# A Mamba front spread over two chunks, its narrow products in column groups, and every scaling with C on GpSimd

## What is computed

```
xz = h @ W_in;  xm, z = split(xz, 2)
xm = silu(causal_conv(xm, conv_w, 4 taps) + conv_b)
dtr, Bm, Cm = split(xm @ W_xp, [64, 80])        # 64 + 16 + 16 columns
dt = softplus(dtr @ W_dt + b_dt);  A = -exp(A_log)
def step(hst, (dt_t, B_t, C_t, x_t)):            # 64 steps, one after the other
    hst = hst * exp(dt_t * A) + (dt_t * x_t) * B_t     # 128 x 512 x 16
    y   = einsum('bds,bs->bd', hst, C_t)
y = (ys + xm * D_param) * silu(z);  out = x + gate * (y @ W_out)
```

## Time and profile before

| | us |
|---|---|
| median of 3 runs | 2333.99 (2333.95 to 2335.63) |
| the profiled execution's own time | 2334.89 |
| its span in the profile | 2333.1 |
| first keep of the scan starts | 620.30 |
| last feed of the scan starts (two in the row) | 2264.66 |

### The profile page before, as it was taken

The page is one execution under the profiler, slowest core; times in us unless marked ns, Lnnn a source line. Parts: engine busy times, 40 slices in busy tenths (PEclk is TensorE's granted clock), DMA queues, the critical chain, the costliest instruction groups (busy, mean ns, idle before and its releaser), DMA issues. The chain is left out here.

```text
span 2333.1 us, 44474 instructions
## 1 busy us (share of the span) xinstructions
PE 2051.4 (88%) x13497; PEld 1579.0 (68%) x13497; DVE 1969.4 (84%) x3686; ACT 1688.3 (72%) x3652; POOL 1635.2 (70%) x1800
## 2 busy tenths in 40 slices
PE   4899999995699999999999999999999999999870
PEld 3566666662467777777777777777777778777760
DVE  2788888884299898989889898989989898988983
ACT  0455555552688888898888879898888979888840
POOL 2799999985667676776767677776767677676530
PEclk8999999996699999999999999999999999999995
DMA  5122212211000000000000000000000000000218
GB/s 142 39 64 64 64 62 63 62 49 36 10 1 19 6 15 6 15 15 6 15 5 19 6 15 8 13 15 6 20 6 15 6 15 15 6 6 6 95 69 288
DMA packets 71471, 80.75 MB, mean 35 GB/s; under 512 B 12227, under 2 KB 63619, under 8 KB 69188
## 3 DMA queue, kind: packets, MB, share of 16 engines
q1 hardware_dynamic: 66052, 69.52, 9.3%
q10 hardware_dynamic: 5184, 8.39, 1.0%
HBM read 44.33 MB, written 33.55 MB: 33 GB/s over the span
## 5 line engine op out<-in xcount | busy, mean ns | idle before, releaser
L632 ACT ACTIVATE decay<-dtT,decay_rate 128x256 f32<-128x256 f32 x2048 | 866.5, 495 | 0.2
L527 PE MATMUL bank<-ident,decay 128*128 128x128 f32 x4096 | 622.4, 275 | 101.6 <-ACT decay L632 56.0
L537 PEld LDWEIGHTS bank<-ident,scaled 128*128 128x128 f32 x4096 | 486.2, 142 | 231.6 <-issue 193.1
L537 PE MATMUL bank<-ident,scaled 128*128 128x128 f32 x4096 | 622.8, 275 | 1.5 <-POOL scaled L452 1.4
L527 PEld LDWEIGHTS bank<-ident,decay 128*128 128x128 f32 x4096 | 471.7, 141 | 143.7 <-ACT decay L632 103.7
L452 POOL TENSOR_SCALAR scaled<-state,bc 128x512 f32<-128x512 f32 x384 | 278.2, 730 | 255.9 <-DVE state L752 209.3
L742 DVE TENSOR_TENSOR bank<-bank,state 128x512 f32<-128x512 f32 x512 | 340.8, 691 | 117.7 <-PE bank L527 111.5
L452 POOL TENSOR_SCALAR scaled<-fresh,bc 128x512 f32<-128x512 f32 x384 | 273.5, 717 | 235.0 <-DVE fresh L752 214.3
L742 DVE TENSOR_TENSOR bank<-bank,fresh 128x512 f32<-128x512 f32 x512 | 340.3, 690 | 58.9 <-PE bank L527 55.4
L752 DVE SCALAR_TENSOR_TENSOR fresh<-dtx,bc,bank 128x512 f32<-128x512 f32 x512 | 356.9, 737 | 0.0
L752 DVE SCALAR_TENSOR_TENSOR state<-dtx,bc,bank 128x512 f32<-128x512 f32 x512 | 356.8, 737 | 0.0
(11 more groups left out here) (139 smaller groups left out, 3617.0 us busy)
## 6 DMA issues: line engine op xcount, KB each, us to landing
xt<-in_x_dram SPq DMA_DIRECT2D x64, 128.0 KB, 2.2
resid<-x SPq DMA_DIRECT2D x64, 128.0 KB, 1.8
normed<-xh SPq DMA_DIRECT2D x64, 128.0 KB, 1.7
xg<-normed SPq DMA_DIRECT2D x64, 128.0 KB, 2.1
ssm_out<-yo SPq DMA_DIRECT2D x32, 256.0 KB, 2.0
fin_r<-resid SPq DMA_DIRECT2D x8, 1024.0 KB, 13.2
mask_bc<-in_mask_BxS_ik_dram SPq DMA_DIRECT2D x64, 64.0 KB, 2.9
fin_y<-ssm_out SPq DMA_DIRECT2D x32, 128.0 KB, 3.0
```

What stands on the lines that cost most here:

```text
L527: mm = pe.transpose(dec_bank[i % DECAY_BANKS][:, m * P:(m + 1) * P], decay[:, i // BLOCK % 2, n % GROUP, m, t % HALF * P:(t % HALF + 1) * ...
L537: mm = pe.matmul(y_bank[t % HALF][:, m * P:(m + 1) * P], scaled[:, i % RING, m * P:(m + 1) * P], ident[:, :], is_transpose=True, start=Fal ...
L632: act.activation(decay[:, block % 2, e // CB, m, :], dtT[par][:, m, half * HTOK:(half + 1) * HTOK], ACT.Exp, scale=decay_rate[:, m, n:n + ...
```

## The change

- `ON_SCALAR` is empty: all 64 scalings of a chunk are POOL's, none ACT's.
- The front of chunk k runs through bodies k - 2 to k. A position in `SLOTS` is 64 times the body, counted from k - 2, plus the slot. Body k - 2 now holds h0, h1 and u0 to u3 in slots 51 to 60 (before 0 to 10 of body k - 1), and the first of the taps, which start in slot 57 on POOL and 62 on DVE (before 6 and 10) and run on into slots 0 to 4 of body k - 1.
- The rest of body k - 1: gating of x in slots 3, 6, 7, 10; dtr in 9 and 13 with out1 between; dt in 16, 20, 25, 29 with bcT and bc between; ln of softplus in slot 31, its POOL part in 33 to 40; z in 32 to 41 (before 14 to 21); x0 to x3 in 46 to 50; tanh of z in 52 (before 55). The gating of z on POOL moves to slots 5 to 15 of body k.
- dtr was 4 products of 64 columns in a row. It is now 2 x 2: two products of one slot write the lower and the upper half of the partitions, and `w_dt`, stacked twice, adds the halves up within the dt products, whose contraction is now 128 deep instead of 64.
- bc was 16 products with xs as weights and 32 columns streaming. Now four products of 32 output rows each (bcT, two a slot, 512 columns) write four partition groups of a side bank, ACT moves them to SBUF, and four products with `eye_sum` (four stacked unit matrices) turn and add them (bc).
- tanh of x goes into dtT instead of `tmp`. There is one more small DMA of W_dt and one more small DVE instruction (`eye_sum`) in the set-up.
- There is one more body without a scan, c = -2, which makes h and u of chunk 0; body -1 makes the rest of chunk 0 and then h and u of chunk 1.

```diff
-ON_SCALAR = (3, 7, 11, 15)
+ON_SCALAR = ()
...
-        SLOTS = dict(zip(JOBS, ((0,), (1,), (3, 4), (5, 6), (7, 8), (9, 10), (11, 12, 13),
-                                (14, 15), (16, 17), (18, 19), (20, 21),
-                                (22, 23, 24, 25), (27,), (29,), (31,), (33,), (35, 36, 37, 38),
-                                (42, 43, 44), (48,), (50,), (52,), (54,))))
+        SLOTS = {"dtr": at(B1, 9, 13), "out1": at(B3, 10, 11, 12), "dt0": at(B1, 16), "bcT": at(B1, 17, 18),
+                 "dt1": at(B1, 20), "bc": at(B1, 22, 23), "dt2": at(B1, 25), "dt3": at(B1, 29),
+                 "z0": at(B1, 32, 33), "z1": at(B1, 34, 35), "z2": at(B1, 37, 38), "z3": at(B1, 39, 41),
+                 "out0": at(B2, 42, 43, 44), "x0": at(B1, 46), "x1": at(B1, 48), "x2": at(B1, 49), "x3": at(B1, 50),
+                 "h0": at(0, 51), "h1": at(0, 52), "u0": at(0, 53, 54), "u1": at(0, 55, 56),
+                 "u2": at(0, 57, 58), "u3": at(0, 59, 60)}
...
-        X_ORDER, X_TANH, X_GATE = (0, 2, 3, 1), (13, 16, 18, 20), (15, 17, 19, 21)
-        MODULATE, CARRY, SOFTPLUS, GATES = (28, 33), 24, 38, 56
+        X_ORDER, X_TANH, X_GATE = (0, 2, 3, 1), at(B1, 1, 4, 5, 8), at(B1, 3, 6, 7, 10)
+        MODULATE, CARRY, LN = at(0, 21, 25), B1 + 18, B1 + 31
+        SOFTPLUS = at(B1, *range(33, 33 + 2 * CB))
+        Z_TANH, Z_GATES = B1 + 52, at(B2, 5, 6, 8, 9, 11, 12, 14, 15)
...
                 elif kind == "dtr":
+                    pe.wait_ge(s_xs, k * CB + 2 * piece + 2)
+                    for g in range(P // DTR):
+                        m = X_ORDER[2 * piece + g]
+                        mm = pe.matmul(side[g * DTR:(g + 1) * DTR, :], w_xp[:, m, 0:DTR], x[:, m, :],
+                                       start=(piece == 0), stop=(piece == pieces - 1), skip_group_check=True)
+                elif kind == "bcT":
+                    for g in (2 * piece, 2 * piece + 1):
+                        mm = pe.matmul(side[g * 2 * DS:(g + 1) * 2 * DS, :], w_xp[:, g, DTR:DTR + 2 * DS],
+                                       x[:, g, :], start=True, stop=True, tile_position=(0, g * 2 * DS))
+                elif kind == "bc":
+                    for t in (2 * piece, 2 * piece + 1):
+                        mm = pe.matmul(side[:, t * 2 * DS:(t + 1) * 2 * DS], bcT[:, t * P:(t + 1) * P], eye_sum[:, :],
+                                       start=True, stop=True)
```

More of the change, by code:

```diff
@@ L256, in build @@
         s_out = sem("out_stored")
-        JOBS = ("h0 h1 u0 u1 u2 u3 out1 z0 z1 z2 z3 "
-                "dtr dt0 dt1 dt2 dt3 bc out0 x0 x1 x2 x3").split()
-        SLOTS = dict(zip(JOBS, ((0,), (1,), (3, 4), (5, 6), (7, 8), (9, 10), (11, 12, 13),
-                                (14, 15), (16, 17), (18, 19), (20, 21),
-                                (22, 23, 24, 25), (27,), (29,), (31,), (33,), (35, 36, 37, 38),
-                                (42, 43, 44), (48,), (50,), (52,), (54,))))
-        POOL_TAPS = [(m, k) for m in (0, 1) for k in range(TAPS - 1)]
@@ L296, in side_turn, with at @@
-        def side_turn(c, job):
-            return product(c, job) % 2, product(c, job) // 2
-        def side_of(c, job):
-            return side_bank[side_turn(c, job)[0]]
-        def filled(eng, c, job):
-            eng.wait_ge(s_side_filled, product(c, job) + 1)
-        def moved(eng, c, job):
-            b, turn = side_turn(c, job)
+        B1, B2, B3 = ITEMS, 2 * ITEMS, 3 * ITEMS
+        def at(start, *slots):
+            return tuple(start + s for s in slots)
+        SLOTS = {"dtr": at(B1, 9, 13), "out1": at(B3, 10, 11, 12), "dt0": at(B1, 16), "bcT": at(B1, 17, 18),
[4 more added lines that the diff above has]
+                 "u2": at(0, 57, 58), "u3": at(0, 59, 60)}
@@ new lines, in build, with chunk_at @@
+        ROWS = {"out1": B3 + 12, "out0": B2 + 44}
+        BODIES = range(-2, CHUNKS + 1)
+        def chunk_at(c, i, position):
+            k = c + 2 - position // ITEMS
+            return k if position % ITEMS == i and 0 <= k < CHUNKS else None
+        SEQUENCE, COMPLETED = {}, {}
+        for c in BODIES:
+            for i in range(ITEMS):
+                for job in SLOTS:
+                    first, last = chunk_at(c, i, SLOTS[job][0]), chunk_at(c, i, SLOTS[job][-1])
+                    if first is not None:
+                        SEQUENCE[job, first] = len(SEQUENCE)
+                    if last is not None:
+                        COMPLETED[job, last] = len(COMPLETED)
@@ L399, in prefetch_resid @@
                         .then_inc(s_fin_r, 16)
-            def body(c, par, post, scan, pre):
-                if pre and c + 2 < CHUNKS:
-                    filled(sp, c, "h1")
-                    apart(sp)
-                    gather(c + 2)
-                if post:
+            for c in BODIES:
+                if scanned(c - 1):
                     store_rows(c - 1, 1)
@@ L409, in body @@
                     prefetch_resid()
-                if scan:
+                if scanned(c):
                     store_rows(c, 0)
-            body(-1, 1, False, False, True)
-            body(0, 0, False, True, True)
-            for c in range(1, CHUNKS + 1):
-                body(c, c % 2, True, c < CHUNKS, c < CHUNKS - 1)
+                if c + 3 < CHUNKS:
+                    filled(sp, c + 2, "h1")
+                    apart(sp)
+                    gather(c + 3)
             final_rows(sp, 0)
@@ L517, in mamba_tensor @@
+            for c in BODIES:
+                for i in range(ITEMS):
+                    slot(c, i)
         def mamba_tensor(pe):
@@ L618, in mamba_tensor, with slot @@
-            mamba_bodies(pe, body)
+            SKIPS = [index_of(0, t) + LAG - 1 for t in range(T)]
+            def slot(c, i):
+                if i + 2 < ITEMS:
+                    if scanned(c):
+                        turn_decay(c, i + 2)
+                elif scanned(c + 1):
+                    turn_decay(c + 1, i + 2 - ITEMS)
+                if scanned(c) and i in SKIPS:
+                    skip_term(c, SKIPS.index(i))
+                for job in SLOTS:
+                    for piece, position in enumerate(SLOTS[job]):
+                        k = chunk_at(c, i, position)
+                        if k is not None:
+                            fill(k, job, piece)
+                if i >= LAG and scanned(c):
+                    sum_state(c, i - LAG)
+                if i < LAG and scanned(c - 1):
+                    sum_state(c - 1, i - LAG + ITEMS)
```

463 lines of the change are left out of this document (232 added, 231 removed).

## The result

| | before | after |
|---|---|---|
| median, us | 2334.81 (2333.95 to 2338.54, 4 runs) | 2355.49 (2351.51 to 2358.59, 4 runs) |
| the profiled execution's own time, its span | 2334.89, 2333.1 | 2358.59, 2356.8 |
| first keep of the scan starts | 620.30 | 636.67 |
| period of a chunk | 103.9 | 105.1 |

The ratio is 1.0085, with an interval of 1.0064 to 1.0105. The changed kernel is 0.9% slower, 20.7 us. The forecast was 2335, with "slower" as the likeliest sign. 2355 lies inside the whole range (2304 to 2378), but 3 us above the one that the forecast case had for itself (2318 to 2352).

The account below looks back on a forecast made before the run. PE's path in slots 10 to 62, then DVE's heavy stretch, would bound the kernel: 2333.1 - 4.5 - 5.8 - 2.1 + 13 = 2333.7 us span, forecast 2335, range 2304 to 2378.

Parts of the forecast that it names:

- the forecast case: Whole kernel: ACT's wait goes, a PE wait of the same size replaces it; 2335 us, range 2318 to 2352, chance 0.64.
- two rivals that did not happen: Column-group products running in sequence, 2378 us, chance 0.11; POOL becoming the last engine, 2365 us, chance 0.10.
- What bounds the kernel, and the new place of the wait: Keeps wait 8.9 us a chunk, the largest part through ACT; afterwards 8 to 10 for PE, in slots 32 to 61.
- Column groups: Narrow products dtr and bcT: two run side by side at one product's cost; PE's work falls 3.6 us a chunk.
- one after the other: Rival: paired narrow products on PE run in sequence, 2.9 us a chunk more, 43 in all, 2378 us; chance 0.11.
- The charge of 1.15: PE's price in us for a slot with two narrow products, 1.00 + 0.09 + 0.06, mode switches included.
- The wait of u0 for h1: Slot 53: PE's u0 waits 1.7 us for ACT's move of h1, behind the tanh of z.
- the term of 13: Start-up before the first keep: 13 us more, about 5 for bcT and bc, 8 for h, u and two taps.
- DVE's heavy stretch, slots 62 to 7: DVE's pairs, taps and gates take 22.2 us while PE has no fill; item 63's turn comes 1.15 us late.
- the 103.1 of the links: Chunk period summed as 2.5 + 75.5 + 1.7 + 1.15 + 22.2 = 103.1 us, taken as 103.6 for lateness.
- Scalings on POOL cost nothing: Sixteen more scalings, 11.7 us a chunk, bring POOL to 86 of 104 us; cost taken as nothing.
- The rival of a DVE nearly unbound: Cheaper column groups and an early tanh shorten PE's path by 1.7 + 1.8 us; 2282 us, chance 0.15.

Follow-up runs that it names:

- the third run: The changed kernel with states 3, 7, 11 and 15 scaled on ACT again, nothing else: 2414.42 us, ratio 1.0336.
- An order that comes near it: The changed kernel with tanh of z in slot 53, DVE's taps in slots 58 to 63 and out0 in slots 61 to 63: 2256.47 us, ratio 0.9666.
- the first placing of the groups: The kernel before with column groups alone, dtr in slots 22 and 25, bcT in 35 and 36, bc in 38 and 39: 2382.9 us, ratio 1.0203.

## Why the prediction came out as it did

By its steps, the changed kernel's profiled execution against a forecast span of 2333.7: it is 2356.8, 23.1 more. First keep: forecast 633.3, measured 636.7, 3.4 of it. The scan from first keep to last feed makes up the other 19.7, nearly all of it in the period: 15 x (105.1 - 103.6) = 22.5, less 1.4 that body 14 saves beyond the forecast (7.2 against 5.8), and less some 1.4 of small terms in the first bodies. That execution is also 3.1 us above the median of the changed kernel.

The wait's new place and the sizes of most terms were forecast; nearly every miss went to the slow side. Of the signs named ahead, two dtr products side by side and the wait of 1.5 to 2 us at each u0 came as put. The period (105.1, not 103 to 104.5), the first keep (636.7, not 630 to 636), the keeps' wait (7.7, not 8 to 10; 8.8 with the move of out0, and up to slot 63) and PE's waits for decays (8.0 us in 1000, not none) fell a little outside, and POOL is at 81% in the scan where 83% was said. That 2355 still lies in the range is in part luck: the upper end stood for two rivals that did not happen, and so did 0.21 of the 0.46 for "slower".

- **What bounds the kernel, and the new place of the wait: right.** ACT's wait went and a PE wait of about the same size took its place: 7.7 us a chunk, most of it in slots 39 to 46 (2.8) and 56 to 63 (4.2). Turns wait only 8.0 us in 1000 for ACT's decays. But the text made ACT the larger part of the old waits, and there it was wrong: with ACT's 16 scalings gone in the old order the keeps still wait 67.5 of 85.7 us in 1000, and the waits that stayed are mostly PE's.
- **Column groups: right.** 1.01 us for two products, undone 1.86. The rival "one after the other" fell by this row. The charge of 1.15 with its switches stood. Averaged over ten chunks, PE goes from the turn of item 12 to that of item 62 in 77.9 us; the sum said 75.5 + 1.7 = 77.2.
- **The wait of u0 for h1: right within the scan.** 1.67 a chunk against 1.7. It was left out of the start, where it is 3.63 us and the clock is at its lower level for part of the u behind it. Without it the term of 13 would have come out about right, by luck. Inside the term, what stands ahead of x3's end was too high (5, measured 3.0, of which 1.1 is there before the first h of all) and h, u and the taps too low (8, measured 13.4 with the wait).
- **DVE's heavy stretch, slots 62 to 7: mis-sized.** Within the period it is the term that failed most. With item 63's turn it was put at 23.4 and measures 24.2, from the keep of slot 62 to that of slot 8. The text took a tap of about 1.1 as "a contended price already". It was the price of the old overlap, mostly with POOL's scalings of taps; in the new one every second tap meets a POOL add. Now a tap takes (1265.06 - 1262.56) / 2 = 1.25 from start to start, six of them 7.4 against 6.4; item 63's wait was 0.85 instead of 1.15. The contended gate of slot 10 (1.8 us) reaches PE's path too: item 18's turn starts right behind the feed of item 14, 1.16 us after the turn before it and not 0.87, and so costs 0.3.
- **The period, 2.0 above the 103.1 of the links.** 0.8 is the heavy stretch and 0.7 PE's path, 0.3 of it the gate just named. The 2.5 us from the keep of slot 8 to the end of item 12's turn were right (2.1 to its start, 0.44 for the turn), but 0.4 between the end of item 62's turn and its keep stood in no term. The last 0.1 is one long chunk, the eleventh (last section). The text knew that "each link can only be late" and allowed 0.5 for it; it was 0.9 without the contention.
- **Scalings on POOL cost nothing: right.** POOL is not last. In the whole run the sums wait 1.2 us for its scaled states (a row of the page, below). That ACT would have stood the new order with its scalings, as I held before the third run, was wrong by 54 us. And in the old order they give 21 us by ACT's relief alone. The prediction had ACT's path summed up, but never asked what each part would give by itself.

```profile
L541 PE MATMUL bank<-ident,scaled 128*128 128x128 f32 x4096 | 635.5, 279 | 1.3 <-POOL scaled L447 1.2
```

- **The rival of a DVE nearly unbound** did not happen in this kernel. An order that comes near it exists (2256), and not cheaper products bring it, but work of PE and DVE put where the other engine is the slower one. The prediction had named the place ("the empty slots 62 to 7 stay"); filling it with out0 alone gave 41 us.

## What to carry to other kernels

When engines run a fixed order and hand each other four buffers, the sum of each engine's work says little: write down, for each stretch, which engine is slower there, and put every movable piece on the other one. Here moving 3.5 us of PE work into DVE's heavy stretch was worth 41 us over the run, while PE relieved by the groups in the old order, where ACT was last, gained nothing. When one product needs another's result moved by a second engine, look at what stands ahead of that move in the second engine's program, once in the loop and once in the start-up code: the tanh of z stood there, and the logarithm in the first placing of the groups.

Undo or do each part of a bundled change alone before believing in the bundle. One of the three parts, an empty table, was worth more than all of them.
